# A software-pipelined transformer stage: full-array products in four stretches a turn, a fourth rotary buffer, one rotary product moved to the preceding turn

## The chip, the cores and the metric

One core of a Trainium2 chip runs the whole program, in one launch. The metric is the device time of an execution in microseconds. Engine names in the profile: PE is TensorE (PEld its weight loads), DVE is VectorE, ACT is ScalarE, POOL is GpSimd, SP is the engine that issues the DMAs.

## The reference

The input is 16 sequences of 256 tokens with 128 channels. Four blocks follow, each of the form x = x + block(layernorm(x)): a time-mixing block, a gated feed-forward block with ternary weights, an attention block with 16 heads, and last a stack of six layers. Only this last one is changed. Cut to what matters, with `shift_tokens` moving half of the channels by one token:

```python
for i in range(6):                                  # DEPTH
    x = attn_layer(shift_tokens(x), Wqkv[i], ...) + x
    x = ffn_layer(shift_tokens(x), g[i], bln[i], W1[i], b1[i], W2[i], b2[i]) + x

# attn_layer: q, k, v = x @ Wqkv, 16 heads of 64
q = l2norm(q) * qs;  k = l2norm(k) * ksc
q = q * cos * scale + rotate_half(q) * sin * scale
k = k * cos / scale + rotate_half(k) * sin / scale
# windows of 32 tokens, each sees its own and the one before
attn = softmax(where(mask, -max, q @ k.T * 8));  out = (attn @ v) @ Wo
# ffn_layer: layernorm, then (a * gelu(gate)) @ W2 + b2
```

## The kernel before, in words

All activations stay in the core's memory (`x_all`). The last stage (phase d) treats one sequence of one layer as an item n, 96 items in all (6 layers by 16 sequences), in a software pipeline written out by hand. One loop runs over f, the turn (`TURNS_D`, 100 turns), in four functions, one for each of TensorE, VectorE, ScalarE and GpSimd (L1602, L1783, L1863, L2076). A turn works on five items at once: the projection of item f starts, that of f-1 ends, the scores, softmax and value products of f-2, the attention sum of f-3 with the start of its feed-forward part, and the rest of the feed-forward part of f-4. Every call in these loops is a step that waits on semaphores and then issues; an engine executes its steps strictly in the order written. So the lists of calls are the schedule.

The steps that the change and the prediction touch:

- `project(n, i)` (L1900, matmul L1910): queries and keys, in 8 chunks of 2 x 128 columns, six matmuls of the full 128 x 128 array each, in a rounded 32-bit type. Chunks 0 to 3 are keys, 4 to 7 queries. Chunk i goes to bank i % 2, so it waits for the rotary product of chunk i-2.
- `squares(n, i)` (ScalarE, L1680) squares the chunk from the bank; `add_halves` (GpSimd, L1843) adds them; `sum_squares` (TensorE, L1921), `norm_rsqrt`, `norm_weight` (L1456), `norm_factor` (VectorE, L1462), `norm_high` (ScalarE, L1671), `norm_split` (VectorE, L1469) and `spread_norms` (TensorE, L1932) make the factor of the keys and queries, `scale_keys` (VectorE, L1484) applies it to the keys.
- `rotary_products(n, i)` (VectorE, L1448) multiplies the chunk, after its squares, by two tables into a buffer `d_t[c % KS]`, KS = 3; `rotary_sums` (GpSimd, L1835) adds its halves and frees the buffer. rotary sum 0 also waits for the DMAs that place the previous item's keys.
- `place_keys`, `place_queries` (L2151, L2160): eight DMAs each, on SP's queue, between the chunks' layout and that of the scores.
- `scores(n, h)` (L1943 mask, L1950), `attention(n, h)` (L1995), `token_products(n, w)` (w = 0 to 7, L1977) and `sum_squares` are tiled: four matmuls on a quarter of the array's columns each (`128*32` in the profile). All other matmuls use the full array (`128*128`): `turn_tokens` (L1897), `ffn_up` (L2037), `project`, `ffn_tokens` (L2006), `spread_norms`, `ffn_mean` (L2017), `ffn_var` (L2023), `ffn_down` (L2050).
- `token_products(n, w)` alternate between banks 5 and 4; product 2 writes the bank of product 0 and waits for ScalarE's `read_products(n, 0)` (L1704). Products 0 and 1 also wait for `ffn_gate` 1 and 2 (VectorE, L1549) of item f-4, product 6 for `ffn_scale` (VectorE, L1541).
- softmax: `softmax_maximum` (VectorE, L1490), `softmax_shift` (VectorE, L1496), `scale_shifted` (GpSimd, L1852), `softmax_exp` (ScalarE, L1696), `softmax_sum` (VectorE, L1503), `softmax_reciprocal` (VectorE, L1509), `softmax_scale` (GpSimd, L1858), `turn_probabilities` (VectorE, L1516), each for two halves h.
- `split_low_tokens` (VectorE, L1436), which project 0 waits for; `residual` (VectorE, L1523).
- `ffn_residual` (VectorE, L1557) reads bank 6, which the next turn's `turn_tokens` writes; it waits for the count of `s_x_done`.
- At a change of layer ScalarE also makes the new tables (L1764) and the rounded weights (L1752), in two successive turns, and two turns later `head_matrices` come in.

TensorE's order in a turn before: turn_tokens, ffn_up 0 and 1, scores 0, project 5, attention 0, project 6, ffn_up 2, project 7, scores 1, sum_squares 1, attention 1, token product 0, project 0 and 1 of item f, token products 1 and 2, ffn_tokens, spread_norms 0, token products 3 and 4, spread_norms 1, ffn_mean, project 2 and 3, ffn_var, ffn_down, project 4, token product 5, sum_squares 0, token products 6 and 7. The waits that order it with VectorE are in these lines:

```python
# project: the bank of chunk c is free
at_least(pe, s_rp, c - 1)
# rotary_products: squares made, a buffer free
dve.wait_ge(s_sq, c + 1)
at_least(dve, s_ad, c - KS + 1)
# token_products, w < 5: the bank's last product is read
pe.wait_ge(s_uev, u_read + w - 1)
# turn_tokens: bank 6 is free
at_least(pe, s_x_done, n - 4)
```

Of the kernel before, what the change touches and what calls it, by code (L numbers as in the profile page):

```python
# [71 lines left out]
def build(nc, dram, out):  # L72
    ctx = ExitStack()
    with ctx:
# [1241 lines left out]
        QUADS = H // 4  # L1316
        NF = len(FBLK)
        CHUNKS = 8
        KS = 3
        d_xt = [ld(T) for _ in range(3)]  # L1320
        d_sq = [ld(2, T) for _ in range(4)]
        d_t = [ld(2, 2, T) for _ in range(KS)]
        d_rot = [ld(4, 2, T) for _ in range(2)]
# [39 lines left out]
        def here(n):  # L1363

            return 0 <= n <= LAST
# [60 lines left out]
        def phase_d_vector(dve):  # L1426
# [12 lines left out]
            def rotary_products(n, *chunks):  # L1439
                if not here(n):  # L1440
                    return
                for i in chunks:
                    c = CHUNKS * n + i
                    dve.wait_ge(s_sq, c + 1)
                    at_least(dve, s_ad, c - KS + 1)
                    if i % 4 == 0 and n % SEQS == 0:
                        dve.wait_ge(s_tab, 8 * layer_of(n) + i + 4)
                    nc.vector.tensor_tensor(d_t[c % KS].rearrange("p k h t -> p k (h t)"),  # L1448
                                            bank[c % 2][:, :].unsqueeze(1).to_broadcast([P, 2, 2 * T]),
                                            tab[:, i // 4, :, :, :].rearrange("p k h t -> p k (h t)"), ALU.mult).then_inc(s_rp, 1)  # L1450
# [26 lines left out]
            def scale_keys(n, h):  # L1477
                if not here(n):
                    return
                dve.wait_ge(s_R, 2 * n + h + 1)  # L1480
                dve.wait_ge(s_ad, CHUNKS * n + 2 * h + 2)
                rot = d_rot[0][:, 2 * h:2 * h + 2]
                factor = bank[7][:, :].rearrange("p (g t) -> p g t", g=2).unsqueeze(2).to_broadcast([P, 2, 2, T])
                nc.vector.tensor_tensor(rot, rot, factor, ALU.mult).then_inc(s_mR, 1)  # L1484

            def softmax_maximum(n, h):
                if not here(n):
                    return
                dve.wait_ge(s_s, 2 * n + h + 1)
                marks["max", h, n] = link.put(nc.vector.tensor_reduce(out=d_mx[h], in_=score_banks, op=ALU.max, axis=AXX))  # L1490

            def softmax_shift(n, h):
                if not here(n):
                    return
                link.wait(marks["max", h, n])
                nc.vector.tensor_tensor(d_e[h], score_banks, d_mx[h].unsqueeze(2).to_broadcast([P, 4 * QUADS, 2 * WIN]), ALU.subtract)\  # L1496
                    .then_inc(s_sub, 1)
# [45 lines left out]
            def ffn_gate(n, c):  # L1543
                if not here(n):
                    return
                m = FBLK[c]
                dve.wait_ge(s_gl, NF * n + c + 1)
                at_least(dve, s_ffo, n)
                nc.vector.scalar_tensor_tensor(d_h[0:m, c, :], bank[UP_BANK[c]][0:m, T:2 * T], cols_of(n)[0:m, 2 + c:3 + c],  # L1549
                                               d_gl[0:m, c % 2, :], ALU.add, ALU.mult).then_inc(s_h, 1)  # L1550
# [50 lines left out]
            dve.wait_ge(s_stats, 13)  # L1601
            for f in range(TURNS_D):  # L1602
                turn_probabilities(f - 3, 1)
                rotary_products(f - 1, 3)
                ffn_gate(f - 4, 0)
                rotary_products(f - 1, 4)
                softmax_maximum(f - 2, 0)
                rotary_products(f - 1, 5)
                softmax_shift(f - 2, 0)
                rotary_products(f - 1, 6, 7)  # L1610
                ffn_gate(f - 4, 1)
                softmax_maximum(f - 2, 1)
                split_low_tokens(f)
                ffn_gate(f - 4, 2)
                norm_weight(f - 1)
                residual(f - 3)
                norm_factor(f - 1)
                rotary_products(f, 0)
                norm_split(f - 1)
                softmax_shift(f - 2, 1)  # L1620
                scale_keys(f - 1, 0)
                rotary_products(f, 1)
                scale_keys(f - 1, 1)
                softmax_sum(f - 2, 0)
                rotary_products(f, 2)
                ffn_weight(f - 3)
                softmax_reciprocal(f - 2, 0)
                ffn_factor(f - 3)
                ffn_scale(f - 3)
                softmax_sum(f - 2, 1)  # L1630
                softmax_reciprocal(f - 2, 1)
                if f - 4 == LAST:
                    add_kept(3, SEQS - 4, SEQS - 1)
                ffn_residual(f - 4)
                turn_factors(f - 1)
                turn_probabilities(f - 2, 0)
                if f < 2:
                    normalise(*range(3 + 7 * f, min(10 + 7 * f, SEQS)))
                done = f - 4 - SEQS * (LAYERS - 1)
                if done > 0 and done % 4 == 0:  # L1640
                    add_kept(done // 4 - 1, done - 4, done)
# [3 lines left out]
        def phase_d_scalar(act):  # L1645
# [137 lines left out]
            for f in range(TURNS_D):  # L1783
                fresh = here(f) and f % SEQS == 0
                next_fresh = here(f + 1) and (f + 1) % SEQS == 0
                read_products(f - 3, 7)
                read_tokens(f)
                split_high_tokens(f)
                nc.scalar.preload_act_table(ACT.Gelu)
                ffn_gelu(f - 4, 0)  # L1790
                squares(f - 1, 5, 6)
                ffn_gelu(f - 4, 1)
                squares(f - 1, 7)
                ffn_gelu(f - 4, 2)
                nc.scalar.preload_act_table_set(EXP_SET)
                norm_rsqrt(f - 1)
                if fresh:
                    tables(layer_of(f), 0)
                softmax_exp(f - 2, 0)
                if here(f - 2) and (f - 2) % SEQS == 0:  # L1800
                    head_matrices(layer_of(f - 2))
                squares(f, 0)
                norm_high(f - 1)
                read_products(f - 2, 0, 1, 2)
                squares(f, 1)
                if fresh and f:
                    weights_high(layer_of(f), 4, 5, 6, 7)
                ffn_tokens(f - 3)
                read_products(f - 2, 3)
                ffn_square(f - 3)  # L1810
                read_products(f - 2, 4)
                squares(f, 2, 3)
                if fresh:
                    tables(layer_of(f), 1)
                if next_fresh:
                    weights_high(layer_of(f + 1), 0, 1, 2, 3)
                ffn_rsqrt(f - 3)
                softmax_exp(f - 2, 1)
                read_products(f - 2, 5)
                ffn_shift(f - 3)  # L1820
                squares(f, 4)
                read_products(f - 2, 6)
# [61 lines left out]
        def phase_d_tensor(pe):  # L1884
# [191 lines left out]
            for f in range(TURNS_D):  # L2076
                if f == 1:
                    pe.wait_ge(s_stats, 13)
                turn_tokens(f)
                ffn_up(f - 4, 0)  # L2080
                ffn_up(f - 4, 1)
                scores(f - 2, 0)
                project(f - 1, 5)
                attention(f - 3, 0)
                project(f - 1, 6)
                ffn_up(f - 4, 2)
                project(f - 1, 7)
                scores(f - 2, 1)
                sum_squares(f - 1, 1)
                attention(f - 3, 1)  # L2090
                if here(f - 2) and (f - 2) % SEQS == 0:
                    head_matrices(layer_of(f - 2), 0, 1, 2, 3)
                token_products(f - 2, 0)
                project(f, 0, 1)
                token_products(f - 2, 1)
                token_products(f - 2, 2)
                ffn_tokens(f - 3)
                spread_norms(f - 1, 0)
                token_products(f - 2, 3)
                token_products(f - 2, 4)  # L2100
                spread_norms(f - 1, 1)
                ffn_mean(f - 3)
                project(f, 2, 3)
                ffn_var(f - 3)
                ffn_down(f - 4)
                project(f, 4)
                token_products(f - 2, 5)
                sum_squares(f, 0)
                token_products(f - 2, 6)
                token_products(f - 2, 7)  # L2110
# [285 lines left out]
```

## Time and profile before

| | us |
|---|---|
| median of 3 runs | 4239.45 (4238.14 to 4240.38) |
| the profiled execution | 4246.35 |
| its span, first to last instruction | 4244.5 |
| first turn of the last stage starts | 1322.8 |
| an ordinary turn of the last stage | 29.20 |

| engine | busy us | share of the span |
|---|---|---|
| TensorE matmul | 3910.8 | 92% |
| TensorE weight loads | 2747.8 | 65% |
| VectorE | 3529.0 | 83% |
| ScalarE | 2638.6 | 62% |
| GpSimd | 2381.6 | 56% |

The span covers all four stages; the last one takes the time from 1322.8 us on. Busy shares are averages over the stages; within the last stage they are read from the stretches. Ends of matmuls are modelled, so durations on TensorE are best taken from start to start. Successive instructions of VectorE and ScalarE overlap by about 0.1 us in the records, so here too the time that one more instruction in a row takes is that from start to start.

### The profile page before, as it was taken

The numbers are of one execution on the slowest core, as the hardware profiler recorded it, in microseconds if no ns is written. First come the engines' busy times: TensorE is split into PE (matmuls) and PEld (weight loads), VectorE is DVE, ScalarE is ACT, GpSimd is POOL, SyncE is SP. The second block draws the span as 40 slices with busy tenths as digits, with TensorE's granted clock in tenths as the row PEclk, the third lists the DMA queues.
The fourth block names the chain that finished last, engine by engine and source line by source line (L and its number), as shares of the span: only waits on it lengthen the run. The fifth ranks groups of instructions, "written<-read, shape, count | busy, mean of one in ns | idle before, by whom it ended". The sixth has DMA issues, their size and how long they took to land.

```text
span 4244.5 us, 120128 instructions
## 1 busy us (share of the span) xinstructions
PE 3910.8 (92%) x48128; PEld 2747.8 (65%) x48128; DVE 3529.0 (83%) x5537; ACT 2638.6 (62%) x5550; POOL 2381.6 (56%) x2045
## 2 busy tenths in 40 slices
PE   3457999999995999999999999999999999999998
PEld 1225776767764676667766676667766676667666
DVE  6875556777776899989998899989998899989897
ACT  3543336666664666666667666666666666666665
POOL 0111001000003787878888788878888787878785
PEclk7678999999997999999999999999999999999999
DMA  3000000000001333333332333333332333333332
GB/s 104 0 0 1 1 1 1 1 0 0 0 1 40 76 90 82 69 76 88 78 78 65 79 88 81 70 75 94 73 81 62 81 87 81 71 73 72 91 77 65
DMA packets 264482, 238.94 MB, mean 56 GB/s; under 512 B 31524, under 2 KB 260136, under 8 KB 263208
## 3 DMA queue, kind: packets, MB, share of 16 engines
q1 hardware_dynamic: 263976, 231.82, 23.5%
q8 instruction: 363, 5.95, 0.6%
q14 instruction: 143, 1.17, 0.1%
HBM read 26.20 MB, written 4.19 MB: 7 GB/s over the span
## 4 chain that ended last, share of the span: by engine, by line
PE 73%; DVE 12%; ACT 7%; issue 3%; SPq 2%; POOL 1%; DMA 1%; DVEq 0%; ACTq 0%; POOLq 0%
PE bank L1977 14%; PE bank L1910 13%; PE bank L1995 8%; PE bank L1950 7%; PE bank L2037 5%; PE bank L854 5%; ACT arena L1129 3%; PE bank L2050 2%; PE bank L1943 2%; DVE arena L1016 2%; PE bank L1921 2%; DVE arena L1026 2%; PE bank L1254 1%; SPq L2151 1%; PE bank L1245 1%
## 5 line engine op out<-in xcount | busy, mean ns | idle before, releaser
L1448 DVE TENSOR_TENSOR arena<-bank,tab 128x1024 f32<-128x1024 f32 x768 | 935.5, 1219 | 193.0 <-ACT arena L1680 138.8
L1835 POOL TENSOR_TENSOR arena<-arena 128x512 f32<-128x512 f32 x768 | 1010.7, 1332 | 49.6 <-DMA arena<-arena 44.9
L1680 ACT ACTIVATE arena<-bank 128x512 f32<-128x512 f32 x768 | 457.9, 596 | 538.9 <-PE bank L1910 530.1
L1977 PE MATMUL bank<-m_vo,arena 128*32 128x512 f32 x6144 | 757.9, 599 | 17.4 <-DVE arena L1541 11.1
L1910 PE MATMUL bank<-x_split,wqk_split 128*128 128x256 f32 x4608 | 720.7, 299 | 34.9 <-DVE arena L1448 21.0
L1910 PEld LDWEIGHTS bank<-x_split,wqk_split 128*128 128x128 f32 x4608 | 605.6, 192 | 184.3 <-issue 93.9
L1843 POOL TENSOR_TENSOR arena<-arena 128x256 f32<-128x256 f32 x768 | 558.6, 739 | 159.4 <-ACT arena L1680 158.7
L1704 ACT ACTIVATE arena<-bank 128x512 f32<-128x512 f32 x768 | 456.8, 596 | 186.9 <-PE bank L1977 184.2
L1852 POOL TENSOR_TENSOR arena<-arena 128x1024 f32<-128x1024 f32 x192 | 372.4, 1940 | 263.2 <-DVE arena L1496 263.2
L1187 POOL TENSOR_TENSOR x_all<-x_all,arena 128x256 f32<-128x256 f32 x16 | 11.6, 727 | 836.5 <-DVE arena L1008 836.5
L1858 POOL TENSOR_TENSOR arena<-arena 128x1024 f32<-128x1024 f32 x192 | 373.5, 1946 | 127.0 <-DVE arena L1509 126.7
L1950 PE MATMUL bank<-arena 128*32 128x128 f32 x12288 | 403.7, 273 | 0.0
L1995 PE MATMUL bank<-arena 128*32 128x128 f32 x12288 | 373.6, 274 | 0.6 <-issue 0.5
L1950 PEld LDWEIGHTS bank<-arena 128*32 128x32 f32 x12288 | 345.6, 110 | 36.9 <-issue 0.5
L1995 PEld LDWEIGHTS bank<-arena 128*32 128x32 f32 x12288 | 332.7, 110 | 32.5 <-issue 2.0
L1977 PEld LDWEIGHTS bank<-m_vo,arena 128*32 128x32 f32 x6144 | 159.5, 109 | 260.1 <-ACT arena L1704 140.6
L1129 ACT ACTIVATE arena<-bank,arena 128x256 f32<-128x256 f32 x512 | 235.4, 472 | 130.9 <-DVE arena L1016 128.7
L2037 PE MATMUL bank<-arena,w 128*128 128x256 f32 (+1 forms) x1152 | 282.0, 381 | 0.8 <-ACT arena L1735 0.8
L1516 DVE STREAM_TRANSPOSE arena<-arena 128x1024 f32<-128x1024 f32 x192 | 235.1, 1224 | 25.8 <-POOL arena L1858 25.8
L1490 DVE TENSOR_REDUCE arena<-bank 128x16 f32<-128x1024 f32 x192 | 234.1, 1219 | 12.0 <-PE bank L1950 4.1
L1484 DVE TENSOR_TENSOR arena<-arena,bank 128x1024 f32<-128x1024 f32 x192 | 232.1, 1209 | 3.0 <-PE bank L1932 3.0
L1496 DVE TENSOR_TENSOR arena<-bank,arena 128x1024 f32<-128x1024 f32 x192 | 233.0, 1214 | 0.0
(258 smaller groups left out, 7159.4 us busy)
## 6 DMA issues: line engine op xcount, KB each, us to landing
arena<-arena SPq DMA_DIRECT2D x1536, 128.0 KB, 2.5
wqk_stage<-in_wqk SPq DMA_DIRECT2D x6, 1024.0 KB, 8.6
out_x<-x_all SPq DMA_DIRECT2D x7, 512.0 KB, 6.0
wvt<-in_wvt SPq DMA_DIRECT2D x6, 512.0 KB, 4.4
wo<-in_wo SPq DMA_DIRECT2D x6, 512.0 KB, 5.5
arena<-in_wbh SPq DMA_DIRECT2D x1, 2048.0 KB, 9.7
w<-in_w SPq DMA_DIRECT2D x6, 341.0 KB, 5.9
wqk_stage<-out_x SPq DMA_DIRECT2D x2, 512.0 KB, 5.0
```

Source lines behind the costliest of these rows:

```text
L1448: nc.vector.tensor_tensor(d_t[c % KS].rearrange("p k h t -> p k (h t)"), bank[c % 2][:, :].unsqueeze(1).to_broadcast([P, 2, 2 * T]), tab[: ...
L1680: nc.scalar.activation(d_sq[i % 4].rearrange("p h t -> p (h t)"), bank[c % 2][:, :], ACT.Square).then_inc(s_sq, 1)
L1704: nc.scalar.activation(d_u[:, 1 + w, :, :], bank[U_BANK[w]][:, :].rearrange("p (a c) -> p a c", a=QUADS), ACT.Copy).then_inc(s_uev, 1)
L1835: nc.gpsimd.tensor_tensor(d_rot[i // 4][:, i % 4, :, :], t[:, :, 0, :], t[:, :, 1, :], ALU.add).then_inc(s_ad, 1)
L1843: nc.gpsimd.tensor_tensor(sq[:, 0, :], sq[:, 0, :], sq[:, 1, :], ALU.add).then_inc(s_sa, 1)
L1852: nc.gpsimd.tensor_tensor(e, e, factor.to_broadcast([P, WPT, QUADS, 2 * WIN]), ALU.mult).then_inc(s_rm, 1)
L1858: nc.gpsimd.tensor_tensor(d_e[h], d_e[h], d_inv[h].unsqueeze(2).to_broadcast([P, 4 * QUADS, 2 * WIN]), ALU.mult)\
L1910: last = nc.tensor.matmul(bank[c % 2][:, h * T:(h + 1) * T], wqk_split[:, i, wp, h, :], x_split[:, n % 2, xp, :], start=(q == 0), stop=(q ...
L1950: last = nc.tensor.matmul(bank[2 + b][g * WIN:(g + 1) * WIN, (2 * v + a) * P:(2 * v + a + 1) * P], d_q[:, a, g, at:at + WIN], d_k[:, a, g, ...
L1977: last = nc.tensor.matmul(bank[U_BANK[w]][g * WIN:(g + 1) * WIN, :], d_xt[n % 3][:, w * WIN:(w + 1) * WIN], m_vo[:, 4 * g:4 * g + 4, :].re ...
L1995: last = nc.tensor.matmul(bank[6][v * WIN:(v + 1) * WIN, h * C:(h + 1) * C], d_pt[h][:, at, :], d_u[:, WPT * h + v + z, r, :], start=(r == ...
L2037: last = nc.tensor.matmul(bank[UP_BANK[c]][0:m, half * T:(half + 1) * T], w1_of(n)[:, first + c * P:first + c * P + m], d_xn, start=True, ...
```

## The change

Three of the four lists of steps are reordered, and `KS`, the number of rotary buffers, goes from 3 to 4.

- TensorE: project 5 comes before scores 0, next to ffn_up 0 and 1; project 0 and 1 come after token products 1 and 2, next to ffn_tokens. Runs of full-array work in a turn: six before, four after.
- VectorE: rotary 3 of item f comes at the end of turn f, behind ffn_scale, in place of turn f+1. Rotary 4 and 5 come one place earlier. ffn_gate 2 comes before softmax_maximum 1. Rotary 0 comes behind norm_split and softmax_shift 1.
- ScalarE: read_products 0 comes before norm_high; squares 0 and 1 come after read_products 1 and 2.

GpSimd's list and the DMAs' order stay.

```diff
--- before.py
+++ after.py
@@ -1316,7 +1316,7 @@
         QUADS = H // 4
         NF = len(FBLK)
         CHUNKS = 8
-        KS = 3
+        KS = 4
         d_xt = [ld(T) for _ in range(3)]
         d_sq = [ld(2, T) for _ in range(4)]
         d_t = [ld(2, 2, T) for _ in range(KS)]
@@ -1601,23 +1601,22 @@
             dve.wait_ge(s_stats, 13)
             for f in range(TURNS_D):
                 turn_probabilities(f - 3, 1)
-                rotary_products(f - 1, 3)
+                rotary_products(f - 1, 4)
                 ffn_gate(f - 4, 0)
-                rotary_products(f - 1, 4)
+                rotary_products(f - 1, 5)
                 softmax_maximum(f - 2, 0)
-                rotary_products(f - 1, 5)
                 softmax_shift(f - 2, 0)
                 rotary_products(f - 1, 6, 7)
                 ffn_gate(f - 4, 1)
+                ffn_gate(f - 4, 2)
                 softmax_maximum(f - 2, 1)
                 split_low_tokens(f)
-                ffn_gate(f - 4, 2)
                 norm_weight(f - 1)
                 residual(f - 3)
                 norm_factor(f - 1)
-                rotary_products(f, 0)
                 norm_split(f - 1)
                 softmax_shift(f - 2, 1)
+                rotary_products(f, 0)
                 scale_keys(f - 1, 0)
                 rotary_products(f, 1)
                 scale_keys(f - 1, 1)
@@ -1627,6 +1626,7 @@
                 softmax_reciprocal(f - 2, 0)
                 ffn_factor(f - 3)
                 ffn_scale(f - 3)
+                rotary_products(f, 3)
                 softmax_sum(f - 2, 1)
                 softmax_reciprocal(f - 2, 1)
                 if f - 4 == LAST:
@@ -1799,10 +1799,10 @@
                 softmax_exp(f - 2, 0)
                 if here(f - 2) and (f - 2) % SEQS == 0:
                     head_matrices(layer_of(f - 2))
-                squares(f, 0)
+                read_products(f - 2, 0)
                 norm_high(f - 1)
-                read_products(f - 2, 0, 1, 2)
-                squares(f, 1)
+                read_products(f - 2, 1, 2)
+                squares(f, 0, 1)
                 if fresh and f:
                     weights_high(layer_of(f), 4, 5, 6, 7)
                 ffn_tokens(f - 3)
@@ -2079,8 +2079,8 @@
                 turn_tokens(f)
                 ffn_up(f - 4, 0)
                 ffn_up(f - 4, 1)
+                project(f - 1, 5)
                 scores(f - 2, 0)
-                project(f - 1, 5)
                 attention(f - 3, 0)
                 project(f - 1, 6)
                 ffn_up(f - 4, 2)
@@ -2091,9 +2091,9 @@
                 if here(f - 2) and (f - 2) % SEQS == 0:
                     head_matrices(layer_of(f - 2), 0, 1, 2, 3)
                 token_products(f - 2, 0)
-                project(f, 0, 1)
                 token_products(f - 2, 1)
                 token_products(f - 2, 2)
+                project(f, 0, 1)
                 ffn_tokens(f - 3)
                 spread_norms(f - 1, 0)
                 token_products(f - 2, 3)
```

## Rows read from the trace of the kernel before

**Rows 1.** The page's chain that ended last, shares of the span by engine.

```profile
PE 73%; DVE 12%; ACT 7%; issue 3%; SPq 2%; POOL 1%; DMA 1%; DVEq 0%; ACTq 0%; POOLq 0%
```

**Rows 2.** Stretches: start:end, us, then busy us (instructions) by engine, clock, DMA, GB/s.

```profile
1634.09:1663.66 29.57, 29.13 (x441) 20.49 (x437) 26.97 (x34) 19.77 (x37) 23.69 (x21) 1.00 0.32 73
2618.32:2647.52 29.20, 29.07 (x440) 20.46 (x436) 26.96 (x34) 19.78 (x37) 23.70 (x21) 1.00 0.35 78
2736.30:2768.00 31.70, 29.50 (x440) 20.41 (x437) 27.09 (x34) 24.14 (x50) 26.36 (x25) 1.00 0.30 68
```

**Rows 3.** Timeline of the turn 2618.32 to 2647.52, TensorE: start, duration, line, shapes.

```profile
2618.32 0.44 PE L1897 MATMUL bank<-ident,x_all 128*128 128x128 f32 x2
...
2620.42 0.40 PE L1943 MATMUL bank<-mask_bf,ident_bf 128*32 128x512 bf16 x4
...
2622.71 0.97 PE L1910 MATMUL bank<-x_split,wqk_split 128*128 128x256 f32 x6
...
2623.62 1.95 PE L1995 MATMUL bank<-arena 128*32 128x128 f32 x64
...
2625.50 0.98 PE L1910 MATMUL bank<-x_split,wqk_split 128*128 128x256 f32 x6
...
2627.98 0.40 PE L1943 MATMUL bank<-mask_bf,ident_bf 128*32 128x512 bf16 x4
...
2630.17 0.60 PE L1921 MATMUL bank<-arena,sel 128*32 128x256 f32 x8
...
2632.35 1.03 PE L1977 MATMUL bank<-m_vo,arena 128*32 128x512 f32 x8
...
2633.31 1.69 PE L1910 MATMUL bank<-x_split,wqk_split 128*128 128x256 f32 x12
...
2634.93 1.92 PE L1977 MATMUL bank<-m_vo,arena 128*32 128x512 f32 x16
...
2643.51 0.94 PE L1910 MATMUL bank<-x_split,wqk_split 128*128 128x256 f32 x6
```

**Rows 4.** The same turn on the other engines, with idle time before and its releaser.

```profile
2621.28 1.23 DVE L1448 TENSOR_TENSOR arena<-bank,tab 128x1024 f32<-128x1024 f32 x1 [0.96 <-POOL arena L1835]
...
2630.70 1.94 POOL L1852 TENSOR_TENSOR arena<-arena 128x1024 f32<-128x1024 f32 x1
...
2631.57 1.35 DVE L1436 TENSOR_TENSOR x_split<-arena,x_split 128x256 fp32r<-128x256 f32 x1
...
2632.67 1.06 ACT L1696 ACTIVATE arena<-arena 128x1024 f32<-128x1024 f32 x1 [0.53 <-POOL arena L1852]
...
2634.33 0.60 ACT L1680 ACTIVATE arena<-bank 128x512 f32<-128x512 f32 x1 [0.60 <-PE bank L1910]
...
2634.96 1.22 DVE L1448 TENSOR_TENSOR arena<-bank,tab 128x1024 f32<-128x1024 f32 x1 [0.61 <-ACT arena L1680]
2635.13 0.59 ACT L1704 ACTIVATE arena<-bank 128x512 f32<-128x512 f32 x1
...
2635.77 0.18 PEld L1977 LDWEIGHTS bank<-m_vo,arena 128*32 128x32 f32 x8 [0.68 <-ACT arena L1704]
...
2636.10 0.47 DVE L1469 SCALAR_TENSOR_TENSOR z_split<-z_split,odd,arena 128x256 fp32r<-128x256 f32 x1
...
2637.63 1.21 DVE L1484 TENSOR_TENSOR arena<-arena,bank 128x1024 f32<-128x1024 f32 x1
...
2642.15 1.21 DVE L1448 TENSOR_TENSOR arena<-bank,tab 128x1024 f32<-128x1024 f32 x1
...
2644.37 0.48 DVE L1541 SCALAR_TENSOR_TENSOR arena<-bank,cols_d,arena 128x256 f32<-128x256 f32 x1
...
2646.18 0.36 DVE L1557 TENSOR_TENSOR x_all<-x_all,bank 128x256 f32<-128x256 f32 x1
```

**Rows 5.** Timeline at the end of a turn before a change of layer.

```profile
2735.58 0.36 DVE L1557 TENSOR_TENSOR x_all<-x_all,bank 128x256 f32<-128x256 f32 x1
...
2736.25 0.44 PE L1897 MATMUL bank<-ident,x_all 128*128 128x128 f32 x2
```


## The prediction

> **What bounds the kernel now.** I first read the chain that ended last: TensorE carries 73% of it [rows 1]. The table of stretches then gives one ordinary turn of the last stage as 29.20 us (2618.32 to 2647.52), with TensorE busy 29.07, VectorE 26.96, ScalarE 19.78 and GpSimd 23.70 at a full granted clock [rows 2]. So TensorE has no slack but VectorE has little more than 2 us. The timeline of that turn [rows 3, 4] shows what ties them; below, "at x" is the time from its start, 2618.32. TensorE runs through, but project(f,4) at 25.19 starts 0.15 after rotary_products(f,2) ends at 25.04 [rows 3, 4]: VectorE sets this point. From 16.64 (rotary 0) to 25.04 VectorE doesn't pause, and rotary 0 waits for squares 0, which waits for project(f,0) at 14.99. So the turn is already held by a loop over both engines: project 0, squares 0, rotary 0, the row of VectorE work up to rotary 2, project 4, the next turn, project 0. VectorE's slack lies elsewhere: 0.96 before rotary 3, 0.61 before rotary 0 [rows 4].
>
> **The change, part by part.**
>
> *TensorE's stretches.* project 5 alone between tiled work takes 0.91 for six matmuls, project 0 and 1 alone 1.62 for twelve: six more cost 0.71, so going back to tiled work costs 0.20. scores 0 followed by full work takes 2.29, scores 1 followed by tiled work 2.19: 0.10 for the way in [rows 3]. A removed stretch saves 0.30, two save 0.6 in TensorE's own time. project 5 now comes first: scores 0 start at 2.10 + 0.71 = 2.81, and project 6, before at 7.18, starts at 6.86 to 6.88. From there to token product 0 nothing changes in order (6.85), so it starts at 13.71. The Trainium skill (TensorEngine Tiling (Array Packing), Key Properties) says that "changing tiling mode (not just tile) drains the TensorE". The trace agrees, with 0.10 in and 0.20 out. By that rule alone the turn would lose both drains: the second rival below.
>
> *Token products 0, 1, 2 in a row, ahead of project 0.* Product 2 writes the bank of product 0, so it waits for read_products 0 on ScalarE. Before, project 0 and 1 lay between. The read now stands behind softmax_exp 0, and that behind GpSimd's scale_shifted 0 and a chain from project 7's squares. Before, softmax_exp 0 started at 14.35, 7.17 after project 6 [rows 3, 4]; nothing in that chain is reordered, so it starts at 14.03. It takes 1.06, the read 0.59, the load of weights follows 0.05 behind (as 2635.77 follows the read of 2635.13) [rows 4]: with 0.10 of overlap between ScalarE's instructions, product 2 can start at 15.63. TensorE would be ready at 13.71 + 2 x 0.86 = 15.43. (0.86 is a token product in a row, 0.96 less 0.10 for the way out [rows 3].) A wait of 0.20, new. Then project 0 at 15.63 + 0.99 = 16.62; without the wait 16.41.
>
> *Rotary 0, now behind norm_split and softmax_shift 1.* Project 0 to rotary 0 took 16.64 - 14.99 = 1.65; so rotary 0 starts at 18.27. From rotary 0 to rotary 2 it was 25.04 - 1.21 - 16.64 = 7.19, of which norm_split and the shift took 1.53 (2636.10 to 2637.63) [rows 4]. These go ahead of it: 5.66 are left. Rotary 2 starts at 23.93, ends at 25.14: 0.10 later than before, though project 0 is 1.63 later. The moves nearly cancel. norm_split and the shift fit into the gap: VectorE reaches norm_factor about 14.9, ScalarE's norm_high ends at 16.1, and both are done by 18.2 at the latest, counting the lock below. That leaves under 0.1.
>
> *Rotary 3 moved to the end of the turn.* It fills no gap there. From rotary 2's start to ffn_scale's it was 2.22 [rows 4], of which 0.17 waited for ScalarE; the variance comes about 0.2 earlier now, so 2.05. ffn_scale to ffn_residual was 1.81; a rotary product in a row costs 1.13 (1.22 less the overlap). ffn_residual ends at 23.93 + 2.05 + 1.81 + 1.13 + 0.36 = 29.28. The next turn's turn_tokens waits for it, since they share bank 6; with a latency that I estimate at 0.11 (project 4 behind rotary 2 shows 0.15 [rows 3, 4]) it starts at 29.39. By TensorE's own way (project 4 at 25.28 plus the 4.01 up to the next turn) it would be 29.29. Queued behind it: the whole of TensorE, project 5 among it. What was its cover, 1.0 us between ffn_residual's end (28.22) and the turn's, is gone.
>
> *The fourth buffer, rotary 4 first.* Rotary 4 now needs rotary sum 0 as rotary 3 did, and starts at the same 2.97, but TensorE doesn't wait for it before project 6. VectorE then waits for squares 6 and 7 in place of that. So the 0.96 in front [rows 4] becomes idle elsewhere. The gain is in turns whose keys land late: 29.57 in place of 29.20 [rows 2]. About ten such turns at 0.3 each: 3 us. ffn_gate 2 earlier costs nothing: it is 0.4 that moves ahead of softmax_maximum 1, which now has slack for it, and product 1 needs it. The DMA issues aren't moved; keys are placed 0.1 later, queries at about the same point, and scores 0 are 0.7 later, so no price.
>
> *Sum.* An ordinary turn goes from 29.20 to 29.39, bounds 29.09 (no new wait, project 0 + 12.69 as above) and 29.6. There are some 75 ordinary turns of 100 (four at each end and three at each of five changes of layer are not): 75 x 0.19 = +14. In the two slow turns at a change of layer, VectorE's ffn_residual ends 0.31 before the next turn [rows 5], since token product 6 waits for ffn_scale; rotary 3 put behind it costs 1.13 + 0.11 - 0.31 = 0.9 in each: 10 turns, +9. In the turn with head matrices ScalarE is done with softmax_exp 0 long before token product 0, so I take no change there. Late keys -3. Together +20 (bounds -11 and +36). The profiled execution took 4246.35 (span 4244.5) and would take 4266; it stands 6.9 above the median of 4239.45, so the time forecast is 4239.45 + 20 = 4259.
>
> **The rivals.**
>
> *Slower still: the reads of SBUF.* In this trace split_low_tokens, with two inputs in SBUF, started at 13.25 and took 1.35, ending 0.28 after GpSimd's scale_shifted 0 ended at 14.32 [rows 4]; it waited for it. norm_split, also with two such inputs, ran at 17.78 with GpSimd idle. In the new order it starts at 16.2, in the middle of rotary sum 7, and by the same 0.28 ends near 17.1 instead of 16.6. By my times the shift then ends at 18.2, just ahead of rotary 0. From 0.1 more on each further delay goes into rotary 0 and the turn: 0.3 a turn more, 75 x 0.3 = 22, 4282. The Trainium skill (SBUF — State Buffer, Who interferes with whom) states that an instruction of VectorE with two SBUF inputs and one of GpSimd that reads SBUF block each other for the whole instruction. The trace agrees (the 1.35).
>
> *Faster: TensorE keeps what it saves.* By the drains alone a turn would take 29.20 - 0.60 = 28.6, 75 x 0.6 = 45 less, 4194. Against it stands the loop: project 0 can't start before 16.41 and project 4 comes 1.65 + 5.66 + 1.21 + 0.15 = 8.67 later, then 4.01 to the next turn, 29.09. If neither new wait shows, ScalarE's nor ffn_residual's, this gives 75 x 0.11 = 8 less, and 3 for late keys: 4228.
>
> *No change.* If product 2 doesn't wait for the read (softmax_exp 0 0.2 earlier than I make it), a turn takes 29.18; the layer changes cost 9, late keys give 3, together 4239.45 + 4 = 4243.
>
> *The change does not do what it says.* The full stretches could keep their price if it belonged to waits and not to the switch. Then project 6 is 0.3 later and a turn takes 29.7: it falls within the slower cases.
>
> **The numbers.** A measurement of this kernel tells 0.2% (8.5 us) from no change. Forecast 4259 and its neighbours, 4250 to 4270: 0.52. Slower still, about 4282: 0.18. No change, around 4243: 0.20. Faster, 4228 or below: 0.10. So faster 0.10, same 0.20, slower 0.70. The range leaves out the faster case and the far end of the slower one: 4238 to 4282.
>
> **What would show it.** Right: two switches between full and tiled work fewer each way in the timeline, project 5 directly behind ffn_up 1; project 6 at about 6.9; a wait of token product 2's weight load for ScalarE's read of about 0.2 beyond the matmul before; rotary 0 at about 18.3; a wait of turn_tokens for ffn_residual; the gap before rotary 3 gone and new ones before rotary 6, 7 and 0; ordinary turns of 29.4. Layer-change turns near 31.2 and 32.7. Wrong: a turn below 29.1 would mean that rotary 0 doesn't hang on project 0 as I have it; no wait at product 2 would mean that softmax_exp 0 isn't bound by GpSimd; norm_split longer than 1 us with rotary 0 waiting on it would make the first rival right.

## The result, and the profile after

| | before | after |
|---|---|---|
| median, range, us | 4239.45 (4238.14 to 4241.57) | 4261.85 (4258.54 to 4264.4) |
| profiled execution / span, us | 4246.35 / 4244.5 | 4262.23 / 4260.5 |
| last stage's first turn starts, us | 1322.82 | 1317.61 |
| ordinary turn, median, us | 29.21 | 29.38 |

Five executions each; the ratio is 1.0048, with an interval of [1.0037, 1.0059]. The change made the kernel slower by 22.4 us. From the first turn's start to the last one's the last stage took 2837.9 us against 2817.6, 20.3 more; the spans differ by 16.0 only, mainly because this execution came to the stage 5.2 us earlier. So the profiled executions differ by 15.9 us and the medians by 22.4: the one profiled before the change stood 6.9 above its median, the one after it 0.4.

The page of after, its part 4 (first row, as [rows 1]) and two rows of its part 5:

```profile
PE 43%; DVE 33%; issue 10%; ACT 9%; POOL 2%; SPq 1%; DMA 1%; DVEq 0%; ACTq 0%; POOLq 0%
...
L1448 DVE TENSOR_TENSOR arena<-bank,tab 128x1024 f32<-128x1024 f32 x768 | 936.6, 1220 | 101.8 <-ACT arena L1680 86.5
L1835 POOL TENSOR_TENSOR arena<-arena 128x512 f32<-128x512 f32 x768 | 1009.6, 1331 | 13.4 <-DMA arena<-arena 9.8
```

TensorE carried 73% of the chain, now 43%, and VectorE 33% in place of 12%: more of the chain runs over VectorE. Rotary sums, on the other hand, wait less for DMAs: 9.8 us, where the page of before has 44.9. The stretches of an ordinary turn and of the two slow turns at a change of layer (to be held against [rows 2]):

```profile
2625.74:2655.11 29.37, 28.74 (x436) 20.67 (x437) 27.68 (x34) 19.77 (x37) 23.64 (x21) 1.00 0.33 74
...
2713.88:2744.93 31.05, 28.94 (x437) 20.64 (x437) 28.35 (x34) 21.81 (x42) 26.46 (x25) 1.00 0.31 70
2744.93:2777.55 32.62, 29.03 (x436) 20.70 (x437) 27.32 (x34) 24.38 (x50) 26.38 (x25) 1.00 0.29 66
```

TensorE's busy time in the turn fell from 29.07 to 28.74 us, the turn rose from 29.20 to 29.37, and VectorE's busy time rose from 26.96 to 27.68 with the same 34 instructions. TensorE's own timeline of that turn (as [rows 3]):

```profile
2625.74 0.41 PE L1897 MATMUL bank<-ident,x_all 128*128 128x128 f32 x2
...
2627.53 1.06 PE L1910 MATMUL bank<-x_split,wqk_split 128*128 128x256 f32 x6
2628.52 0.40 PE L1943 MATMUL bank<-mask_bf,ident_bf 128*32 128x512 bf16 x4
...
2632.56 0.98 PE L1910 MATMUL bank<-x_split,wqk_split 128*128 128x256 f32 x6
...
2639.41 2.98 PE L1977 MATMUL bank<-m_vo,arena 128*32 128x512 f32 x24
2642.32 1.69 PE L1910 MATMUL bank<-x_split,wqk_split 128*128 128x256 f32 x12
...
2650.98 0.95 PE L1910 MATMUL bank<-x_split,wqk_split 128*128 128x256 f32 x6 [0.42 <-DVE arena L1448]
```

The two stretches are gone: project 5 runs straight behind ffn_up 1, and the three token products stand in one row of 24. Project 6 starts at 6.82 of the turn (7.18 before). The last row shows where the saved time goes: project 4 waits 0.42 us for rotary 2, which ends no earlier than before. The other engines (as [rows 4]; POOL's rows are the ones that VectorE's rows are to be read against):

```profile
2637.77 1.93 POOL L1852 TENSOR_TENSOR arena<-arena 128x1024 f32<-128x1024 f32 x1
2638.84 1.15 DVE L1436 TENSOR_TENSOR x_split<-arena,x_split 128x256 fp32r<-128x256 f32 x1
2639.66 2.89 POOL L1835 TENSOR_TENSOR arena<-arena 128x512 f32<-128x512 f32 x2
2639.73 1.06 ACT L1696 ACTIVATE arena<-arena 128x1024 f32<-128x1024 f32 x1 [0.53 <-POOL arena L1852]
2640.57 0.85 DVE L1462 SCALAR_TENSOR_TENSOR arena<-arena 128x256 f32<-128x256 f32 x1
2641.32 0.16 PEld L1977 LDWEIGHTS bank<-m_vo,arena 128*32 128x32 f32 x8 [0.93 <-ACT arena L1704]
2641.90 0.94 DVE L1469 SCALAR_TENSOR_TENSOR z_split<-z_split,odd,arena 128x256 fp32r<-128x256 f32 x1 [0.48 <-ACT z_split L1671]
2642.76 1.21 DVE L1496 TENSOR_TENSOR arena<-bank,arena 128x1024 f32<-128x1024 f32 x1
2643.33 1.32 ACT L1680 ACTIVATE arena<-bank 128x512 f32<-128x512 f32 x2 [0.27 <-PE bank L1910]
2643.96 1.22 DVE L1448 TENSOR_TENSOR arena<-bank,tab 128x1024 f32<-128x1024 f32 x1
...
2649.62 1.22 DVE L1448 TENSOR_TENSOR arena<-bank,tab 128x1024 f32<-128x1024 f32 x1
2650.18 0.42 ACT L1728 ACTIVATE arena<-arena 128x256 f32<-128x256 f32 x1
...
2654.60 0.36 DVE L1557 TENSOR_TENSOR x_all<-x_all,bank 128x256 f32<-128x256 f32 x1
2655.08 0.20 PEld L1897 LDWEIGHTS bank<-ident,x_all 128*128 128x128 f32 x2 [0.92 <-DVE x_all L1557]
```

VectorE's longer busy time is mostly the lock with GpSimd, of which the prediction's first rival speaks: norm_split takes 0.94 where it took 0.47, norm_factor 0.85 where it took 0.46, split_low_tokens 1.15 where it took 1.35. The last two rows are the end of the turn: ffn_residual ends at 2654.96, the weight load for turn_tokens follows 0.12 behind, the matmul 0.15 behind. The waits from 1500 to 4200 us, of after:

```profile
PEld bank L1897 <- DVE x_all L1557: 82.3, 80, 1.8
...
DVE z_split L1469 <- ACT z_split L1671: 69.1, 90, 5.2
...
PE bank L1910 <- DVE arena L1448: 34.5, 81, 0.8
...
PE bank L1897 <- DVE x_all L1557: 9.0, 10, 0.9
```

and of before, the same groups:

```profile
PEld bank L1897 <- DVE x_all L1557: 9.2, 11, 0.8
PE bank L1910 <- DVE arena L1448: 5.3, 10, 2.9
...
DVE z_split L1469 <- ACT z_split L1671: 0.5, 1, 0.5
```

A wait of turn_tokens for ffn_residual was there in 11 turns. Now the weight load has it in 80, and the matmul itself in ten (9.0 us).

### The profile page after: what moved, and what is told of

The parts are those of the page before. It is cut to its first block, busy times and chain, and to the rows that moved or that the text cites. A ratio compares the mean times of both kernels' runs of the same rounds, so it can differ in the third digit from the quotient of the medians.

```text
span 4260.5 us, 120127 instructions
## 1 busy us (share of the span) xinstructions
PE 3867.3 (91%) x48128; PEld 2757.7 (65%) x48128; DVE 3589.7 (84%) x5537; ACT 2639.8 (62%) x5550; POOL 2373.1 (56%) x2045
## 4 chain that ended last, share of the span: by engine, by line
PE 43%; DVE 33%; issue 10%; ACT 9%; POOL 2%; SPq 1%; DMA 1%; DVEq 0%; ACTq 0%; POOLq 0%
PE bank L1910 7%; PE bank L1977 6%; PE bank L2037 5%; DVE arena L1484 5%; PE bank L854 4%; DVE arena L1448 4%; PE bank L1950 4%; PE bank L1995 4%; ACT arena L1129 3%; DVE arena L1503 3%; DVE arena L1496 2%; DVE arena L1016 2%; DVE arena L1490 2%; DVE x_split L1436 2%; DVE arena L1549 2%
## 5 line engine op out<-in xcount | busy, mean ns | idle before, releaser
L1835 POOL TENSOR_TENSOR arena<-arena 128x512 f32<-128x512 f32 x768 | 1009.6, 1331 | 13.4 <-DMA arena<-arena 9.8
```

The lines of the kernel that those rows point to most:

```text
L1835: nc.gpsimd.tensor_tensor(d_rot[i // 4][:, i % 4, :, :], t[:, :, 0, :], t[:, :, 1, :], ALU.add).then_inc(s_ad, 1)
```

## The experiments

Twelve kernels were timed, each beside the kernel before on the same chip; that one's median was 4240.81, 4239.96 and 4240.38 us in three groups of four; the kernel after was timed before them, beside a median of 4239.45. "Turn" is the median distance of two ordinary turns of the profiled execution.

| kernel | us | ratio | turn |
|---|---|---|---|
| 1 after, rotary 3 behind ffn_residual | 4247.31 | [1.0008, 1.0027] | 29.30 |
| 2 first half | 4241.22 | [0.9992, 1.0011] | 29.14 |
| 3 first half, rotary 3 behind ffn_residual | 4218.79 | [0.9936, 0.9964] | 28.88 |
| 4 second half | 4274.34 | [1.0065, 1.0098] | 29.64 |
| 5 after, softmax_exp 0 late | 4262.16 | [1.0035, 1.0069] | 29.43 |
| 6 after, shift 1 ahead of norm_split | 4260.29 | [1.0034, 1.0068] | 29.39 |
| 7 after, 5 and 6 | 4260.31 | [1.0037, 1.0071] | 29.43 |
| 8 before, four buffers | 4236.39 | [0.9979, 0.9998] | 29.21 |
| 9 before, four buffers, rotary 3 to 5 as in 3 | 4248.47 | [1.0014, 1.0035] | 29.35 |
| 10 as 3, rotary 2 ahead of softmax_sum 0 | 4198.41 | [0.9893, 0.9926] | 28.63 |
| 11 as 7, rotary 3 behind ffn_residual | 4225.45 | [0.9949, 0.9977] | 29.14 |
| 12 as 9, rotary 5 behind softmax_maximum 0 | 4236.15 | [0.9983, 1.0002] | 29.21 |

**Does rotary 3 ahead of ffn_residual hold the turn's end?** Experiment 1 moves that one call.

```diff
                 ffn_scale(f - 3)
-                rotary_products(f, 3)
                 softmax_sum(f - 2, 1)
...
                     ffn_residual(f - 4)
+                rotary_products(f, 3)
```

> The changed kernel with rotary 3 four steps later: behind ffn_residual, still in the preceding turn. Theory A (a loop project 0, rotary 0, rotary 2 holds the turn, and its last link is ffn_residual behind rotary 3): turn_tokens no longer waits for ffn_residual, project 4's way decides, an ordinary turn 29.28 us instead of 29.38, the two slow turns at a change of layer back from 31.05 and 32.62 to about 30.3 and 31.8; in all 4247. Rival B (only the late project 0 costs, rotary 3's place nothing): 4262, turns unchanged. Rival C (rotary 3's place is the whole loss): 4240, turns of 29.20.

It took 14.5 us off the changed kernel. The turn falls by 0.08 only, to the 29.30 of the other route (project 4 behind rotary 2, forecast at 29.29); the slow turns at a change of layer fall from 31.05 and 32.62 to 30.1 and 31.7, about 0.95 each. So rotary 3's place costs little in an ordinary turn, where a second route ends just ahead of it (75 x 0.08 are 6 us in all), and 9 us at the changes of layer.

**Which half costs?** The first half is project 5 beside ffn_up, the fourth buffer and rotary 3 to 5 moved. The second is project 0 and 1 behind token product 2, with ScalarE's reads and squares, rotary 0 and ffn_gate 2. Experiment 2 undoes the second half, experiment 4 makes it alone.

```diff
                 token_products(f - 2, 0)
+                project(f, 0, 1)
                 token_products(f - 2, 1)
                 token_products(f - 2, 2)
-                project(f, 0, 1)
```

> Only the first half of the change: project 5 next to ffn_up, four buffers, rotary 3 behind ffn_scale; project 0 and 1 stay between token products 0 and 1, with ScalarE's and VectorE's orders around them as before. Theory A: project 6 at 6.86, project 0 at 14.67, rotary 2 from 23.5, ffn_residual ends at 28.87, ordinary turn 28.98; layer changes still 0.9 longer in two turns each: 4228. Rival B: 28.9 and no cost at the layer changes, 4213. Rival C (rotary 3 is the whole loss): 4258 or more.

> Only the second half, on the kernel before: token products 0 to 2 in a row with project 0 and 1 behind them, read_products 0 ahead on ScalarE, rotary 0 behind the shift, ffn_gate 2 earlier; three buffers, rotary 3 and project 5 where they were. Theory A: project 0 at 16.93 (product 2 waits 0.2 for the read), rotary 0 at 18.6, project 4 at 25.6, ordinary turn 29.6: 4270, slower than the whole change, since the first half's 0.3 is missing. Rival B: 4260. Rival C: 4240 or less.

The second half alone cost 33.5 us: a turn of 29.64, near the forecast. Project 0 starts at 16.98 of its turn, 1.99 later than before, the row from rotary 0 to rotary 2 is only about 1.5 shorter, and project 4 waits 0.42 us for rotary 2, as in the kernel after. The first half alone changed nothing in the time that can be told, where 4228 was expected: its ordinary turns are 0.07 shorter (75 x 0.07 are 5 us), but its slow turns at a change of layer are 30.94 and 32.30 in place of 30.33 and 31.70, 0.6 longer each (6 us). The end of its turn, VectorE and TensorE:

```profile
2637.81 1.22 DVE L1448 TENSOR_TENSOR arena<-bank,tab 128x1024 f32<-128x1024 f32 x1
2639.11 0.42 DVE L1529 SCALAR_TENSOR_TENSOR arena<-bank,arena 128x256 f32<-128x256 f32 x1
...
2642.98 0.36 DVE L1557 TENSOR_TENSOR x_all<-x_all,bank 128x256 f32<-128x256 f32 x1
...
2643.48 0.41 PE L1897 MATMUL bank<-ident,x_all 128*128 128x128 f32 x2 [0.22 <-DVE x_all L1557]
```

ffn_weight (L1529) starts 1.30 behind rotary 2, not 1.13: ScalarE's reciprocal root (L1728) ends 0.06 later than rotary 2, as before the change. My expectation had left this 0.17 out. ffn_residual then ends 0.14 before turn_tokens starts. If that is the whole cause, the gain must appear once rotary 3 is out of the way (experiment 3 makes the moves of 1 and 2 together):

> The first half alone, with rotary 3 behind ffn_residual. Theory A: ordinary turn 28.88 by project 4's way, layer changes as before: 4239 - 24 - 3 = 4212, faster than both kernels by 0.6%. Rival B: the same time as the run without this move. Rival C: 4240.

It did: 28.88, and 4218.79 us, under both kernels. The expected 4212 was too good by 7 (its five executions spread from 4206.83 to 4224.31); the turn was exact.

**Is rotary 0 held by project 0, or by the lock between VectorE and GpSimd?** In the rows of after norm_split takes 0.94 (0.47 before), and the shift starts at 2642.76; with 1.13 from start to start in a row, rotary 0 could start at 2643.89. Squares 0 end at 2643.93, and rotary 0 starts at 2643.96. Two paths meet within 0.07 us. Experiment 5 takes one away (squares 0 come earlier, since softmax_exp 0 is moved behind them and no longer holds read 0), experiment 6 the other (norm_split behind the shift, where it takes 0.47 again), experiment 7 both.

```diff
-                softmax_exp(f - 2, 0)
...
                 squares(f, 0, 1)
+                softmax_exp(f - 2, 0)
```

```diff
                 norm_factor(f - 1)
-                norm_split(f - 1)
                 softmax_shift(f - 2, 1)
+                norm_split(f - 1)
```

> The changed kernel with softmax_exp 0 moved behind squares 0 and 1 on ScalarE, so that read_products 0 no longer stands behind it and token product 2 doesn't wait. Theory A (two paths meet at rotary 0 within 0.1 us: project 0 with its squares, and VectorE's norm_split, held up by GpSimd, with the shift behind it): project 0 0.18 earlier, but rotary 0 only 0.07 earlier, turn 29.31 in place of 29.37. Rival D (the read's wait alone): turn 29.19, 4248. Rival E (the lock alone): 29.37.

> The changed kernel with softmax_shift 1 ahead of norm_split on VectorE, so that norm_split meets GpSimd's rotary sum 7 only at its end and the 0.94 us of norm_split shrink to about 0.5. Theory A: VectorE is ready for rotary 0 about 1 us earlier, rotary 0 still waits for its squares, turn 29.37 as in the changed kernel. Rival D: 29.37. Rival E (the lock alone): 29.2, 4248.

> Both moves: softmax_exp 0 behind the squares, softmax_shift 1 ahead of norm_split. Theory A: now rotary 0 is 0.18 earlier, turn 29.19, 4262 - 14 = 4248. Rival D: the same as with the first move alone. Rival E: the same as with the second move alone.

From the start of their turns rotary 0 came at 18.16, 18.24 and 18.07 (after: 18.22). So the two paths are as read: only both together bring 0.15. In experiment 5 project 0 starts at 16.42, where the forecast has 16.41 without the wait for the read. But none of the three turns became shorter, against what I expected of 5 and 7; those of 5 and 7 are 0.05 longer. The end of experiment 7's turn:

```profile
2646.37 1.22 DVE L1448 TENSOR_TENSOR arena<-bank,tab 128x1024 f32<-128x1024 f32 x1
2647.69 0.42 DVE L1529 SCALAR_TENSOR_TENSOR arena<-bank,arena 128x256 f32<-128x256 f32 x1
...
2651.55 0.36 DVE L1557 TENSOR_TENSOR x_all<-x_all,bank 128x256 f32<-128x256 f32 x1
...
2647.24 0.42 ACT L1728 ACTIVATE arena<-arena 128x256 f32<-128x256 f32 x1
...
2647.73 0.95 PE L1910 MATMUL bank<-x_split,wqk_split 128*128 128x256 f32 x6
...
2652.06 0.41 PE L1897 MATMUL bank<-ident,x_all 128*128 128x128 f32 x2 [0.24 <-DVE x_all L1557]
```

Rotary 2 ends 0.14 earlier and project 4 starts 0.15 earlier, at 25.09. But ffn_weight now waits for L1728, which ends at 2647.66, since softmax_exp 0 has pushed ScalarE's row for the feed-forward part back; ffn_residual ends at 29.28 of the turn (29.22 in the kernel after), and the turn with it 0.05 later. If so, the gain hides behind ffn_residual, and rotary 3 out of its way must show it (experiment 11, the moves of 7 and 1 together):

> The change with softmax_exp 0 behind squares 0 and 1, softmax_shift 1 ahead of norm_split, and rotary 3 behind ffn_residual. Theory (rotary 0 is held by two paths that meet, squares 0 and the shift, and the gain of taking both away was hidden behind ffn_residual): project 4 at 25.09 us of the turn and 4.01 more give a turn of 29.10 us, layer-change turns of 30.1 and 31.6, and 4247 - 75 x 0.19 = 4233 us. Rival (rotary 0's start isn't what sets project 4, or a further wait ends just behind): 29.29, as with rotary 3 behind ffn_residual alone, and 4247.

29.14, against 29.30 with rotary 3's move alone: the two paths at rotary 0 are worth 0.15 a turn. The time is 21.9 us under experiment 1; 75 x 0.15 are 11 of these. In the two profiled executions the last stage differs by 19.8 us; what is not in the ordinary turns lies in the first four (3.5), in the turns with head matrices, two of which were held up in experiment 1 (3.3), and in other turns held up one by one. Why the medians show it too stays open.

**Where does the first half's gain come from: TensorE's switches or VectorE's new order?** Experiment 8 has the fourth buffer alone (`KS = 4`), experiment 9 everything of experiment 3 but the regrouping of project 5, and experiment 12 puts rotary 5 back behind softmax_maximum 0.

```diff
                 scores(f - 2, 0)
                 project(f - 1, 5)
...
-                rotary_products(f - 1, 3)
+                rotary_products(f - 1, 4)
                 ffn_gate(f - 4, 0)
-                rotary_products(f - 1, 4)
+                rotary_products(f - 1, 5)
```

> The kernel before with four buffers and rotary 3 behind ffn_residual, rotary 4 and 5 one place earlier, but project 5 left behind scores 0: nothing is regrouped on TensorE. Theory A (the faster run with the first half alone gains by the two switches it saves between tiled and full work): turn 29.20 as before, 4237. Rival F (it gains by VectorE's freed wait for the rotary buffer): turn 28.9, 4212.

> The kernel before with a fourth rotary buffer and nothing else. Theory (the buffer count binds only where a previous item's keys land late, since rotary 3 and 4 wait for rotary sums 0 and 1 otherwise by 0.96 us of idle time that another wait would replace): ordinary turn 29.20 us as before, 4235 to 4239 us. Rival (VectorE's 0.96 us before rotary 3 was worth time): a turn below 29.1 and a time below 4232.

```diff
                 ffn_gate(f - 4, 0)
-                rotary_products(f - 1, 5)
                 softmax_maximum(f - 2, 0)
+                rotary_products(f - 1, 5)
```

> The kernel with four buffers, rotary 3 behind ffn_residual and no regrouping (29.34 us), with rotary 5 back behind softmax_maximum 0, so that VectorE doesn't wait for squares 5 ahead of it. Theory (the switches of TensorE alone make the 28.88 of the first half): six stretches remain, so a turn takes 29.20 as before, 4238 us. Rival (rotary 3 at the end of the turn gives time whatever TensorE's order): below 29.0, 4222 or less.

Experiment 9 met neither expectation. Its row on VectorE that tells why:

```profile
2681.42 1.22 DVE L1448 TENSOR_TENSOR arena<-bank,tab 128x1024 f32<-128x1024 f32 x1 [1.44 <-ACT arena L1680]
```

This is rotary 5, ahead of softmax_maximum 0 and waiting for squares of a chunk that TensorE makes only after the scores. The shift that frees scores 1's banks ends later, and scores 1 starts 0.14 late. With rotary 5 back (experiment 12) the turn is 29.21, the same as before, with the buffers and the place of rotary 3 of experiment 3. Experiments 12 and 3 still differ in two things, project 5's place and rotary 5's. But the 0.33 between them is there before VectorE can matter: project 6 starts at 7.18 and 6.84, project 0 at 14.99 and 14.65. So it belongs to project 5's regrouping: one switch into tiled work and one out of it, forecast at 0.30. Rotary 5's early place depends on it: experiment 9, which differs from 3 in project 5's place alone, takes 0.47 more. The Trainium skill (TensorEngine Tiling (Array Packing), Key Properties) says that a change of tiling mode drains TensorE; the 0.33 agrees with it, though no run here shows that the price is a drain. Experiment 8 is 4 us under the kernel before, just clear of no change ([0.9979, 0.9998]). In its profiled execution the ordinary turns are 29.21 as before, and two of the 75 were held up, by 0.8 us together, where the kernel before had eleven of 29.4 to 30.1, 4.0 us together. Its rotary sums wait for DMAs as before (35.7 us; before 37.4); the fourth buffer hides the wait.

**How far does the first half go?** In experiment 3 project 4 still waits for rotary 2.

```diff
+                rotary_products(f, 2)
                 softmax_sum(f - 2, 0)
-                rotary_products(f, 2)
```

> The first half of the change with rotary 3 behind ffn_residual (turn 28.88 us), and rotary 2 ahead of softmax_sum 0 as well. In the 28.88 turn project 4 starts 0.15 us behind rotary 2's end (24.71), with TensorE 0.28 later than its own way. Rotary 2 one place earlier (1.13 us) takes this wait away: by TensorE's own way an ordinary turn takes 28.60, 75 turns x 0.28 = 21 us less than the 4218.8 of that kernel: about 4198. Rival (another wait of VectorE or ScalarE ends just behind): 28.75 to 28.85, 4209 to 4217.

Its turn, as a stretch:

```profile
2620.38:2649.02 28.64, 28.64 (x441) 20.53 (x437) 26.92 (x34) 19.68 (x37) 23.66 (x21) 1.00 0.32 73
```

TensorE is busy for the whole of it, as expected of a turn by TensorE's own way. 4198.41 us is the fastest of all, 0.9% under the kernel before.

## Why the prediction was right

4259 was forecast for the median, 4261.85 measured; the direction and the two mechanisms (a later project 0 that the shorter row behind rotary 0 makes up for, and rotary 3 ahead of ffn_residual) hold. By its steps, each from the start of the turn at 2625.74:

| step | forecast | measured |
|---|---|---|
| project 6 | 6.86 to 6.88 | 6.82 |
| token product 0 | 13.71 | 13.67 |
| softmax_exp 0 | 14.03 | 13.99 |
| weights of token product 2, behind read 0 | 15.63 | 15.58 |
| project 0 | 16.62 | 16.58 |
| norm_split's end / the shift's | 17.1 / 18.2 | 17.10 / 18.23 |
| rotary 0 | 18.27 | 18.22 |
| rotary 2 | 23.93 to 25.14 | 23.88 to 25.10 |
| project 4 | 25.28 | 25.24 |
| ffn_residual's end | 29.28 | 29.22 |
| next turn_tokens | 29.39 | 29.37 |
| slow turns at a change of layer | 31.2, 32.7 | 31.05, 32.62 |

- *TensorE's stretches.* Right for project 5: project 6 is 0.36 earlier (0.30 to 0.32 forecast), and experiments 3 and 12 give 0.33 by themselves. Too large for project 0 and 1: from token product 0 to token product 3 TensorE took 5.04 us before and 4.84 in experiments 5, 7 and 11, where product 2 doesn't wait. That is 0.20 where 0.30 was forecast; in the kernel after, with the wait, it is 0.05. The turn doesn't show the difference, since VectorE holds project 4.
- *Token products in a row.* Right: product 2's weights follow read 0, 0.04 behind it.
- *Rotary 0's new place.* Right that the moves nearly cancel: rotary 2 ends 0.06 to 0.07 later than before. So what the first half saves on TensorE ends in the wait of project 4, and experiment 4 shows this half as the one that costs. The row of VectorE's work from rotary 0 to rotary 2 is as long as forecast, 5.66.
- *Rotary 3.* Right in size at the changes of layer: 0.72 and 0.92 a turn, 8 us where 9 was forecast; experiment 1 gives it back. In an ordinary turn its cost is the 0.08 between the two routes, near the forecast (29.39 against 29.29). Two small misses cancel there: ffn_residual ended 0.06 earlier than forecast, and turn_tokens followed 0.15 behind it and not 0.11.
- *Head matrices.* No change was forecast; undisturbed, these turns went from 33.93 to 33.63, five times 0.3: -1.5.
- *The fourth buffer.* Wrong in the kernel after: the -3 for late keys is seen with the fourth buffer alone (experiment 8, 4 us), not here. The rows below are from a turn of 29.80. Rotary sum 0 waits 0.66 for the DMAs, scale_shifted 0 starts at 12.46 of the turn in place of 12.03, and product 2's matmul waits 0.46 for read 0 and comes 0.43 later in its turn than otherwise: this is the very wait that the second half adds. Five turns of 29.58 to 29.80 are held up in this way. Two others took 30.96 and 31.11, which the forecast had no term for (last section): +3.3.

```profile
2116.92 2.53 POOL L1835 TENSOR_TENSOR arena<-arena 128x512 f32<-128x512 f32 x2 [0.66 <-DMA arena<-arena]
...
2127.16 1.93 POOL L1852 TENSOR_TENSOR arena<-arena 128x1024 f32<-128x1024 f32 x1
...
2130.71 1.06 PE L1977 MATMUL bank<-m_vo,arena 128*32 128x512 f32 x8 [0.46 <-ACT arena L1704]
```

For the last stage of the profiled execution, +20 was forecast and 20.3 measured: 75 x 0.18 = +13.4 in ordinary turns, +8.6 at the changes of layer, +2.5 in turns held up one by one, the two long ones included (where the forecast has -3), +0.8 in the first four turns, -2.9 in the turns with head matrices (-1.5 as above, the rest since one fewer of them was held up), and -2.1 in one turn near the end (33.60 before, 31.51 after). That the sum came out this close is partly luck: the late keys that it got wrong are made up for by terms that it didn't have. The profiled execution took 4262.23 where 4266 was forecast, mainly since it came to the stage 5.2 us earlier.

*The rivals.* "Slower still" by the lock had its mechanism and its 0.1 of slack right: norm_split ended 0.28 behind GpSimd's rotary sum, at the time forecast, and the slack, under 0.1 by the forecast, was 0.07 and not used up. The lock hit norm_factor too (0.85 in place of 0.46), which the forecast did not have. The Trainium skill (SBUF — State Buffer, Who interferes with whom) has the rule; the trace agrees with the 0.94 in place of 0.47. Experiment 6 takes the lock at norm_split away and gains nothing by itself, as this reading demands. "Faster" fell with experiment 4: with project 0 moved the loop over rotary 0 takes 0.43 more a turn, and project 5's stretch gives back less than that. "No change" needed product 2 not to wait; it does. Its 29.18 would not have come of it either: experiment 5 takes this wait away, and its turn is 29.43. The shift on VectorE lets rotary 0 come only 0.06 earlier, a limit that the prediction had named but left out of this sum, and ffn_weight then waits for L1728. "The change does not do what it says" fell with project 6 at 6.82.

What the prediction did not see was the order of the next waits. It had the two routes to turn_tokens, 0.10 apart, and the two to rotary 0. Experiments 2, 5 and 7 showed a third place, ffn_weight behind ScalarE's L1728, which ends 0.24 before rotary 2 in the kernel after and 0.07 behind it in experiment 7.

## What to carry to other kernels

Grouping full-array work saved TensorE 0.33 us a turn with project 5 and 0.20 with project 0 and 1. Only the first could shorten the turn: project 0 is the head of a loop over another engine, and moving it later cost more than its stretch gave. Before a step is appended to the end of a software-pipelined turn, ask what the next turn's first instruction waits for, and put the step behind that. When an experiment takes a wait away and nothing happens, take the next one away as well before the theory is given up: here the waits stood 0.07 to 0.24 us apart.

## What the runs showed of the hardware that I had not expected

An instruction of VectorE with two inputs in SBUF can wait for more than one instruction of GpSimd. In the 31.11 us turn of the kernel after:

```profile
2401.82 3.85 DVE L1436 TENSOR_TENSOR x_split<-arena,x_split 128x256 fp32r<-128x256 f32 x1
...
2400.95 1.96 POOL L1852 TENSOR_TENSOR arena<-arena 128x1024 f32<-128x1024 f32 x1
2402.84 2.55 POOL L1835 TENSOR_TENSOR arena<-arena 128x512 f32<-128x512 f32 x2
```

split_low_tokens usually takes 1.15 us there and ends 0.3 after scale_shifted 0, with a rotary sum of GpSimd drawn out behind it (two of them 2.89, where two take 2.55 otherwise). Here it took 3.85, until GpSimd had finished two more instructions in a row (2405.39) plus 0.28. I read this as a gap between GpSimd's instructions that it missed twice. The same happened in the turn of 30.96 (3.70 us), and not once in the profiled execution of the kernel before, where the longest took 1.48. In experiment 10 two took 4.40 and 4.26 us, in turns of 31.33 and 32.76. So an instruction behind this lock can cost a single turn 1.6 to 4 us; what decides whether it gets the gap was not tried.
